# Attention block on one core: scores two groups nearer to their maxima, and new places for the uses of the spare bank

## The reference

```
h = x @ W1 + b1 ; q, k, v per head
w = softmax(causal(q k^T / sqrt(8)))
x = layernorm(x + (w @ v) @ Wp + bp)
xr, xk = mu * x + (1 - mu) * x_prev        (two mixes)
x = layernorm(x + sigmoid(xr @ Wr^T) * (square(relu(xk @ Wk^T)) @ Wv^T))
```

## Time and profile before

| | |
|---|---|
| median of 3 runs | 766.48 us (765.03 to 768.18) |
| the profiled execution: time, span | 766.06 us, 764.3 us |
| busy: PE, DVE, ACT, POOL | 621.4 us (81%), 557.7 (73%), 471.6 (62%), 378.4 (50%) |
| mean granted TensorE clock | 0.959 |
| steps 0 to 14, where T and S both run | some 40.5 us each |

### The profile page before, as it was taken

The page is one execution under the profiler, slowest core; times in us unless marked ns, Lnnn a source line. Parts: engine busy times, 40 slices in busy tenths (PEclk is TensorE's granted clock), DMA queues, the critical chain, the costliest instruction groups (busy, mean ns, idle before and its releaser), DMA issues.

```text
span 764.3 us, 18024 instructions
## 1 busy us (share of the span) xinstructions
PE 621.4 (81%) x6733; PEld 279.5 (37%) x6733; DVE 557.7 (73%) x1644; ACT 471.6 (62%) x918; POOL 378.4 (50%) x520
## 2 busy tenths in 40 slices
PE   2256987998988989898989898988989898977743
PEld 2013233434343435343434434343435343433232
DVE  3067777778888887879797978788887978782231
ACT  1111676586767676677777686767676766677510
POOL 6110334355655655565556464655655565455533
PEclk9999999999999999999999999999999999999755
DMA  1241213132331323241413141332323231100100
GB/s 47 96 97 49 94 54 104 44 92 66 79 93 58 112 58 115 45 124 34 118 38 118 40 127 45 75 96 58 112 59 113 54 104 29 47 17 16 29 14 14
DMA packets 65500, 53.19 MB, mean 70 GB/s; under 512 B 10882, under 2 KB 61316, under 8 KB 65412
## 3 DMA queue, kind: packets, MB, share of 16 engines
q1 hardware_dynamic: 65412, 52.03, 24.5%
HBM read 34.70 MB, written 17.30 MB: 68 GB/s over the span
## 4 chain that ended last, share of the span: by engine, by line
PE 60%; DVE 21%; ACT 8%; issue 5%; POOL 2%; DMA 2%; SPq 1%; POOLq 0%; DVEq 0%; ACTq 0%
PE ops L510 15%; DVE rowmax L661 12%; PE sps L487 10%; PE tps L451 10%; PE spare L390 8%; ACT probs L592 6%; PE spare L404 5%; PE sps L472 3%; DVE h L714 3%; PE spare L430 2%; PE spare L417 2%; PE spare L420 1%; PE spare L402 1%; DVE y L703 1%; PE spare L427 1%
## 5 line engine op out<-in xcount | busy, mean ns | idle before, releaser
L661 DVE TENSOR_REDUCE rowmax<-sps 128x1 f32<-128x512 f32 (+7 forms) x1024 | 401.3, 448 | 103.0 <-PE sps L487 102.2
L592 ACT ACTIVATE probs<-tps 128x512 f32<-128x512 f32 x640 | 346.4, 595 | 149.9 <-PE tps L451 149.9
L761 POOL TENSOR_SCALAR_AFFINE_SELECT probs<-probs 128x512 f32<-128x512 f32 x256 | 158.0, 635 | 272.6 <-ACT probs L592 272.6
L510 PE MATMUL ops<-probs,vop 128*32 128x384 f32 (+3 forms) x2048 | 175.7, 450 | 5.5 <-POOL probs L761 4.2
L451 PE MATMUL tps<-qop,kop 50*128 50x384 bf16 (+3 forms) x1024 | 127.5, 307 | 39.9 <-ACT probs L592 36.1
L487 PE MATMUL sps<-kop,qop 48*64 48x512 bf16 (+7 forms) x2048 | 130.6, 310 | 11.9 <-DMA kop<-d_parts 11.9
L472 PE MATMUL sps<-qmask,dup 64*128 64x128 bf16 (+1 forms) x640 | 69.7, 215 | 38.2 <-DVE rowmax L661 34.0
L451 PEld LDWEIGHTS tps<-qop,kop 50*128 50x128 bf16 x1024 | 34.3, 94 | 164.2 <-ACT probs L592 111.5
L510 PEld LDWEIGHTS ops<-probs,vop 128*32 128x32 f32 x2048 | 50.5, 109 | 79.9 <-issue 61.2
L487 PEld LDWEIGHTS sps<-kop,qop 48*64 48x64 bf16 x2048 | 43.1, 106 | 54.5 <-issue 19.6
L472 PEld LDWEIGHTS sps<-qmask,dup 64*128 64x128 bf16 x640 | 31.4, 95 | 80.6 <-DVE rowmax L661 74.2
(11 more groups left out here) (70 smaller groups left out, 601.7 us busy)
## 6 DMA issues: line engine op xcount, KB each, us to landing
d_parts<-qk_parts SPq DMA_DIRECT2D x16, 768.0 KB, 3.8
qop<-d_parts SPq DMA_DIRECT2D x192, 32.0 KB
qop<-d_parts SPq DMA_DIRECT2D x64, 96.0 KB
kop<-d_parts SPq DMA_DIRECT2D x192, 32.0 KB
kop<-d_parts SPq DMA_DIRECT2D x64, 96.0 KB
xa<-L_attn_x SPq DMA_DIRECT2D x16, 256.0 KB, 3.0
xres<-L_attn_x SPq DMA_DIRECT2D x16, 256.0 KB, 3.4
out<-result SPq DMA_DIRECT2D x16, 256.0 KB, 2.5
```

Source lines behind the costliest of these rows:

```text
L510: last = nc.tensor.matmul(ops[32 * t:32 * t + 32, BLK * a:SEQ], vop[:, par, a, QUARTET * half + t, hh, :], probs[:, g % 2, i, off:off + w] ...
L592: nc.scalar.activation(probs[:, g % 2, i, :], tps[:, bank(4 * GROUPS * n + 4 * g + i), :], ACT.Exp, scale=SCALE)\
L661: last = nc.vector.reduce_max(rowmax[:, par, QUARTET * half + i, a:a + 1], sps[:, bank(n), off:off + w], axis=AX_X)
L761: last = nc.gpsimd.affine_select(out=v, in_=v, compare_op=ALU.is_ge, fill=0.0, base=0, pattern=[[0, QUARTET], [1, BLK]], channel_multiplie ...
```

## The change

T, D and E now run two groups ahead of the step (`LEAD = 2`): in step b and group g they do what belongs to position 10b + g + 2. So T's first group of a batch comes in g8 of the step before, and scores follow maxima by eight groups, not ten. The uses of the spare bank have new places, written in the frame of their stage; in groups of S they go:

| use | before | after |
|---|---|---|
| q, k, v, max0, xT, max1 | g0/1, g1/1, g5/1, g6/0, g6/1, g1/0 | the same |
| sums0, sums1 | g8/1, g2/1 | g8/0, g0/0 |
| attnT, project, hT | g3/1, g5/0, g8/0 | g2/1, g3/1, g7/0 |
| key, gate, value | g2/0, g3/0, g4/1 | g9/1, g2/0, g4/0 |

DVE: the moments of y move from g5 to g4, those of z from g6 to g5, the normalising of h from g7 to g6, that of the result from g9 to g7. ACT: `scale_steps` from g9 to g7, `copy_o` from g6 and g1 to g4 and g9. POOL: `split_max` from g7 and g2 to g6 and g1, `inverse_deviation` from g6 and g7 to g5 and g6, `mix_step` g9 to g7, `mix_sum` g0 to g8, `ksq` g3 to g0, `xbias` g3 to g2, `z` g5 to g4. SP issues xres first in a step. Work, shapes and numbers of instructions are the same. The semaphores of the spare bank are now counted from a table.

```
-    (0, 1): ("A", "q"),
-    (1, 0): ("T", "max1"), (1, 1): ("A", "k"),
-    (2, 0): ("E", "key"), (2, 1): ("D", "sums1"),
-    (3, 0): ("E", "gate"), (3, 1): ("D", "attnT"),
-    (4, 1): ("E", "value"),
-    (5, 0): ("D", "project"), (5, 1): ("S", "v"),
-    (6, 0): ("S", "max0"), (6, 1): ("X", "xT"),
-    (8, 0): ("D", "hT"),
-    (8, 1): ("T", "sums0"),
+    ("X", "xT"): (6, 1),
+    ("A", "q"): (0, 1), ("A", "k"): (1, 1),
+    ("S", "v"): (5, 1), ("S", "max0"): (6, 0),
+    ("T", "max1"): (3, 0),
+    ("D", "sums0"): (0, 0), ("D", "sums1"): (2, 0), ("D", "attnT"): (4, 1), ("D", "project"): (5, 1), ("D", "hT"): (9, 0),
+    ("E", "key"): (1, 1), ("E", "gate"): (4, 0), ("E", "value"): (6, 0),
 }
+LATE = ("T", "D", "E")
+LEAD = 2
...
+def late(b, g):
+
+    t = GROUPS * b + g + LEAD
+    return t // GROUPS, t % GROUPS
...
@@ PE
-            def step(b, par):
+            def step(b):
                 for g in range(GROUPS):
+                    tb, tg = late(b, g)
                     for i in range(0, QUARTET, 2):
-                        if active("T", b):
-                            t_chunks(b, par, g, i)
+                        if active("T", tb):
+                            t_chunks(before("T", tb), tg, i)
                         if active("S", b):
-                            s_masks(b, g, i)
-                            s_chunks(b, 1 - par, g, i)
-                        spare_use(b, par, g, i // 2)
+                            s_masks(before("S", b), g, i)
+                            s_chunks(before("S", b), g, i)
+                        for _, use, n in ORDER[b, g, i // 2]:
+                            spare_use(use, n)
...
@@ DVE
+                    if tg == 6 and active("D", tb):
+                        n = before("D", tb)
+                        is_read(dve, "project", n)
+                        layer_norm_moments(y, 0, n, stats_done, moments_done)
+                    if tg == 7 and active("E", tb):
+                        n = before("E", tb)
+                        wait(dve, z_done, n + 1)
+                        layer_norm_moments(z, 1, n, stats2_done, moments2_done)
+                    if tg == 8 and active("D", tb):
+                        n = before("D", tb)
+                        wait(dve, z_done, n - 1)
+                        normalise(0, n, y, h[:, n % 2], rstd_done, h_done)
+                    if tg == 9 and active("E", tb):
...
@@ POOL
+                    if tg == 7 and active("D", tb):
+                        inverse_deviation(0, before("D", tb), moments_done, vareps_done, rstd_done)
+                    for half, use in enumerate(("max0", "max1")):
+                        for _, due, n in ORDER[b, g, 0]:
+                            if due == use:
+                                split_max(n, half)
+                    if tg == 8 and active("E", tb):
+                        inverse_deviation(1, before("E", tb), moments2_done, vareps2_done, rstd2_done)
```

More of the change, by code:

```diff
@@ L93, in before, with spare_bank, spare_order, spare_counts @@
     return min(max(b + OFFSET[stage], 0), BATCH)
[L96 to L113, removed]
+def late(b, g):
+    t = GROUPS * b + g + LEAD
+    return t // GROUPS, t % GROUPS
+def spare_bank(use, n):
+    return 0
+def spare_order():
+    order = {}
+    for b in range(FIRST_STEP, LAST_STEP + 1):
+        for g in range(GROUPS):
+            for place in range(2):
+                due = [(stage, use, frame) for (stage, use), at in SPARE_USES.items()
+                       for frame, fg in [late(b, g) if stage in LATE else (b, g)]
+                       if at == (fg, place) and active(stage, frame)]
+                assert len(due) <= 1, due
+                order[b, g, place] = [(stage, use, before(stage, frame)) for stage, use, frame in due]
+    return order
+ORDER = spare_order()
+def spare_counts():
+    counts, used = {}, {}
+    for uses in ORDER.values():
+        for _, use, n in uses:
+            k = spare_bank(use, n)
+            counts[use, n] = used.get(k, 0)
+            used[k] = counts[use, n] + 1
+    return counts
+COUNTS = spare_counts()
 def exp_chunk(c, i):
@@ L319, in load_max @@
                             .then_inc(max_in[half], 16)
-            def step(b, par):
-                other = 1 - par
+            def step(b):
+                par, other = b % 2, 1 - b % 2
+                if active("D", b):
+                    wait(sp, xbias_done, before("D", b))
+                    sp.dma_start(xres[:], x[b + OFFSET["D"]].rearrange("(t p) e -> p t e", p=P)).then_inc(xres_in, 16)
                 if active("S", b):
@@ L392, in tokens_by_weights, with spare_use @@
                 return last
[L394 to L398, removed]
+            def spare_use(use, n):
+                k, par = spare_bank(use, n), n % 2
+                spare = spares[k]
+                wait(pe, spare_read[k], COUNTS[use, n])
                 if use == "xT":
-                    wait(pe, xa_in, 16 * (before("X", b) + 1))
+                    wait(pe, xa_in, 16 * (n + 1))
                     for t in range(TT):
@@ L545, in _, with spare_use @@
             act.wait_ge(armed, 1)
-            def spare_use(b, par, g, place):
-                stage, use = SPARE_USES.get((g, place), (None, None))
-                if stage is None or not active(stage, b) or use in ("sums0", "sums1", "project", "value"):
+            def spare_use(use, n):
+                if use in ("sums0", "sums1", "project", "value"):
                     return
-                n = before(stage, b)
+                k, par = spare_bank(use, n), n % 2
+                spare = spares[k]
                 if use in ("max0", "max1"):
-                    m = 2 * n + (0 if use == "max0" else 1)
-                    wait(act, max_split, m)
-                wait(act, spare_written, spare_before(b, use) + 1)
+                    wait(act, max_split, 2 * n + int(use[-1]))
+                is_written(act, use, n)
                 if use == "xT":
-                    ins = nc.scalar.copy(xT[:, 1 - par], spare[:])
+                    ins = nc.scalar.copy(xT[:, par], spare[:])
                 elif use == "v":
@@ L673, in layer_norm_moments, with spare_use @@
                 last.then_inc(done_moments, 1)
-            def spare_use(b, par, g, place):
-                stage, use = SPARE_USES.get((g, place), (None, None))
-                if stage is None or not active(stage, b):
+            def spare_use(use, n):
+                if use not in ("q", "k", "sums0", "sums1", "project", "value"):
                     return
-                n = before(stage, b)
-                written = spare_before(b, use) + 1
+                k = spare_bank(use, n)
+                spare = spares[k]
                 if use in ("q", "k"):
```

283 lines of the change are left out of this document (139 added, 144 removed).

## The result

The changed kernel takes 805.92 us, median of 4 runs (799.56 to 810.31), against 767.33 (765.03 to 768.26) for the kernel before on the same chip: a ratio of 1.0501, interval 1.0407 to 1.0595. It is 5% slower. 757.0 was predicted, with a range of 747 to 766, so the prediction was wrong in sign and by 48.9 us, and its slow case with the nearest cause (769.7) was far too small.

The account below looks back on a forecast made before the run. No engine alone was taken as the bound: PE works 36.27 of 40.53 us a step, DVE 34.37. Terms -3.6 + 1.3 - 6.2 - 1.0 = -9.5 on 766.06 gave 756.6, as median 757.0 us; range 747 to 766.

Parts of the forecast that it names:

- slow case with the nearest cause: DVE's full stretch, g4 to g9, grows as normalising meets POOL's work: 0.2 to 0.8 us a step, 769.7; chance 0.12.
- `normalise`: DVE's normalising of h (1.3) and result (1.6): 2.9 us together, no change; both slow 3.4; -0.7 to +0.6 a step.
- The rule that it weighed: DVE's tensor_scalar and POOL exclude each other: h waiting out a 1.05 us pow makes 13 us over 13 steps; chance 0.04.
- The walk of g0: Start of a step, sums1 in place 0: 0.73 + 0.58 + 0.75 + 1.06 (q) + 1.00 = 4.12 us.
- g9's key on the path: Last group of a step: key, moved from g2, lengthens g9 from 2.73 to 4.21 us, +1.48.
- The move of g4: In g4, value in place 0 covers the wait for ACT: 3.23 us against 3.81 before, -0.58.
- The 1.3 us for h: DVE's normalising of h in g6, beside POOL's small splits and the pow of z, takes 1.3 us.
- The start: First steps, T joining at S's g8: 21.2 us against 17.02, some 3 saved by the clock, +1.3 (+0.7 to +3.5).
- the rival with 0.08: T waits for maxima whose loads land 3 us after issue: 0.5 to 1 us a step on PE, 764 to 770; chance 0.08.
- the rival with 0.12: DVE's stretch g4 to g9 grows as h and result meet POOL's streaming work: 769.7 at +0.7 a step; chance 0.12.
- The end: After the full steps: two T groups saved, -6.2 us, and sums0 hidden less hT's delay, -1.0 us (0 to -2).
- the cancelling of y and gated: In the tail, project no longer waits behind value, but gated and z precede y's moments and h's pow: 0 in all.

Follow-up runs that it names:

- busy_stall: The changed kernel with 18 transposes added on PE at the start of g8, written into the free spare bank: 784.9 us, ratio 1.0206.
- res_g9: The changed kernel with the normalising of the result moved on DVE from g7 to g9: 751.2 us, ratio 0.9799; measured again 748.3 us.
- res_g8: The changed kernel with the normalising of the result moved on DVE from g7 to g8: 789.31 us, ratio 1.0276.
- res_split: The changed kernel with tiles 0 and 1 of the result normalised in g7, tiles 2 and 3 in g9: 760.28 us, ratio 0.9898.
- before_res_mixsum: The kernel before with the result normalised in g0 of the next step, beside POOL's mix sum, not in g9: 808.14 us, ratio 1.0529.

## Why the prediction was wrong

**The failed term: `normalise`.** The prediction took 1.6 us for the result "since POOL does the same streaming work as before and only its partner changes", with bounds of 1.11 and 1.7 from its rows. It measured 3.45. The sum over both (2.9, at most 3.4) was 4.73. What it got wrong is that POOL's work is not a load that slows DVE by a share of its own. In these runs it is a row of instructions of which each part of the result sits one out, so what counts is how many stand there without a gap, and how long they are. One is the least that a part can lose: in the kernel before, h starts at 390.75, and its second part takes 1.04 us, since it sits out both the end of the small split (to 391.37) and the whole mask behind it (0.63). That is what made 1.72 of 1.11 there, and the trace of the kernel before could have told it. The two instructions of `mix_sum`, 1.25 us each, are among the longest on POOL. The prediction set "the last mask and `mix_step`" beside the result and left them out, as they stand in g8 of POOL's program; POOL was early enough to run the first of them beside it. The bounds came from rows in which POOL had gaps, and could not show this; the timeline of POOL in g7 after the change could be worked out (hT's copy, step difference, masks, `mixed`, all within 4.7 us), and the prediction did work it out, but for POOL's own deadlines only.

**The rule that it weighed.** The Trainium skill (SBUF — State Buffer, Who interferes with whom) says that of a VectorE instruction in a two-port mode, which `tensor_scalar` can enter, and a GpSimd one, whichever issues first holds the port pair that they share and keeps the other out until it ends. The prediction took the tail's row, h at 1.11 beside a pow, as the case against it and gave it 0.04. By this case's rows the rule fits masks, step difference and `mixed`: 3.45 in g7, 1.63 for half of it, 2.60 beside `mixed` and a mask, 1.11 in a gap. It doesn't show for the pow of 4 elements a partition: after the change too, the parts of h that run beside it take 0.34 us each, in g6 (pow from 408.90) and in the tail. Nor does it show for other forms of DVE's work: row maxima of 128x512 out of PSUM (0.69 us) and the statistics of y and z (`BATCH_NORM_STATS2`, 0.28) take the same with POOL at its long instructions and without. The error was to settle the rule by its exception, and to price it only for h.

**The cost with no term: the clock.** The prediction priced a wait of PE as its length. PE's 2.80 us of idling in g8 were followed by 3.4 to 10.2 us at half clock in every one of the 13 steps. busy_stall puts this apart: 21.0 us of the loss are gone when PE is kept busy in the same wait. No rival had it. Without it the loss would have been 784.9 - 767.9 = 17.0 us, by the same-chip times.

**The wait for q.** The walk of g0 had 1.06 for q and nothing for the bank: sums1 moved to place 0 of the same group, DVE reads it after both chunks, and PE stands for 0.97 us in each of 13 steps, 12.6 in all. The prediction asked of max1 whether it waits for the read before it ("as before"), and didn't ask it of q, whose predecessor is new.

**What was right.** The eight other groups, sum 31.87 against 31.67 measured; g9's key on the path there (4.21 against 3.99). The move of g4 (3.23, measured 3.26). The 1.3 us for h (1.28). No wait of PE for POOL, ACT or SP grew into the step, and the maxima cost PE 1.3 us in the whole run, so the rival with 0.08 (0.5 to 1 us a step) is excluded. The sign by which it would be wrong, steps over 41 us with L749 beside POOL as the place to look (L714 before), led straight to the cause, and the rival with 0.12 had its direction. The start came to 87.81 at T-and-S's g2 instead of 86.37, +1.4 against +1.3, but by another sum: everything ran 1.2 us later even before T joined (the masks of S's g7 at 67.17, not 65.94), and the rest of the walk was that much too dear. That 1.2 isn't the change's: the runs differ by it before T joins (q of step -1 at 42.56 here and 41.33 before, but 41.23 in busy_stall and 41.52 in res_g9). So +1.4 against +1.3 is luck. The clock was up at 83.0, where about 82 was given.

**The end** gained 9.34 after S's last scores, where -6.2 - 1.0 = -7.2 was predicted. The windows show the two parts, up to T's last chunks and after them; first before, then after:

```profile
683.05:716.80 33.75, 26.81 (x241) 11.12 (x239) 10.23 (x42) 25.10 (x50) 20.08 (x29) 0.90 0.06 17
716.80:764.30 47.50, 20.23 (x92) 12.97 (x92) 10.39 (x46) 8.18 (x14) 16.82 (x18) 0.55 0.08 23
```

```profile
736.59:760.70 24.11, 20.06 (x191) 8.57 (x187) 8.05 (x32) 19.16 (x39) 14.31 (x22) 1.00 0.01 2
760.70:808.50 47.80, 20.91 (x96) 13.42 (x96) 11.73 (x51) 8.72 (x15) 18.13 (x20) 0.55 0.08 23
```

T's part is 9.64 us shorter. The clock in it is 1.00 where it was 0.90: T is now through before the clock falls. That is the likely source of the 2 us that no step of the prediction had; no run sets it apart. What follows T is the same to 0.3 us, as the cancelling of y and gated had it. Two slips in the working cost nothing: the terms given for g9 add up to 4.11, and to 4.21 only with the 0.1 us from its price list, and "both as slow as h was" is +0.5 us a step, not +0.6.

**The sum put right**, per step: 40.25 + 1.85 (result) + 0.97 (q) = 43.07, measured without half clock 43.09; with the clock's 2.3, 45.35. Taken over 13 steps the three misses are 24, 13 and 30 us, together 67, more than the miss of 48.9 in the median. Counted by spans, the miss is 44.2 + 9.5 = 53.7. The eleven full steps make 52.9 of it and not 56, since the kernel before had half clock of its own in its mean of 40.81; the last 1.9 steps make 3.9, and the ends gave 3.1 back. The other 4.8 are the medians': the profiled execution is at the slow end of its runs (810.26 of 799.56 to 810.31). The runs' times go with their half clock: the granted clock is 0.925 and 0.926 in the two of 810, 0.934 and 0.941 in those of 801.59 and 799.56. By the medians the clock's part is 21 of the 38.6 us lost, by the periods of the profiled execution up to 30.

**Left open.** What decides whether an idle stretch of PE brings half clock: 2.0 to 2.8 us did in every step of the changed kernel and about 1.53 in twelve of thirteen of res_g8, 1.15 in three of thirteen of the kernel before, 0.98 in one of res_split; what PE did around them differs too, and some stretches begin with no idling over 0.46 us in the 10 us before them. Why a part of h was passed over twice where parts of the result were passed over once is open, and so is the exclusion for `tensor_scalar` of other types or from PSUM, which no run has.

## What to carry to other kernels

When an elementwise instruction of VectorE on SBUF moves, draw GpSimd's timeline at the new place and count the instructions that stand there without a gap: each part of it sat out at least one here, so put it where GpSimd idles (1.11 us in the gap, 3.45 in the row). Ask also which DMA issue waits for it: in before_res_mixsum the store of the result held up the loads behind it in SP's queue. A wait of TensorE in a loop that is otherwise busy is to be priced twice, for its length and for the half clock that may follow it; work that fills it can pay for itself. And when uses of one bank change their order, ask for each use, not only for the moved ones, who must have read the bank before it.

## What was not expected of the hardware

- A DVE `tensor_scalar` of 128x128 f32, 0.34 us alone, took up to 1.317 us beside POOL's instructions of 128x512 f32 (1.25 each), and four of them 3.45 us; the same four took 1.11 with POOL idle for 2.50 us, and in the tail the four of h took 1.11 with POOL at a pow of 128x4.
- 18 transposes added to each of 14 steps made the kernel 21.0 us faster (805.92 to 784.9), as the granted clock between the start and the tail stayed at 2.4 GHz for all but 6.8 us instead of all but 78.5.
- Moving four DVE instructions in the kernel before (before_res_mixsum) cost 5.3%, though a step without half clock or late masks grew by only 1.75 us. The store that waits for them held SP's queue, xres came late, `pv` waited up to 2.83 us for its masks, and 64.9 us at half clock came on top (20.5 before).
